# Where the "other nodes' edges" penalty of an attention maximum is added: from an activation and a fused add-and-max to a matmul that accumulates in the same bank

## The chip, the cores and the metric

The kernel runs on one core of one Trainium2 chip. A core has a matrix engine (TensorE, PE in the rows, its weight loads PEld), VectorE (DVE), ScalarE (ACT), GpSimd (POOL) and a queue engine (SyncE, SP) that issues transfers. The metric is device time in microseconds (us). Three timed runs of the kernel before gave a median of 5694.3 us, from 5691.99 to 5695.6 us.

## The reference, cut to what matters

Four graph layers run one after another on 3125 nodes and 100000 edges. The change lies in the first, which holds four rounds of attention over the edges. Each round computes, per edge, a score, and then a softmax over the edges that share a source node:

```
qi = Q[src]; kj = K[dst]
score = (qi * kj).sum(-1) + 0.1 * (edge_attr * qi[:, :RBF]).sum(-1) + logm[dst]
smax  = jax.ops.segment_max(score, src, num_segments=N)
es    = jnp.exp(jnp.minimum(score - smax[src], 20.0))
denom = jax.ops.segment_sum(es, src, num_segments=N)
alpha = es / (denom[src] + 1e-10)
```

What the change touches is `smax`: the maximum of the scores over the edges of each source node.

## The kernel before, in words

Nodes are cut into NB = 25 blocks of P = 128. The edges of a block of source nodes are stored in KT = 38 columns of 128 edges each. For every block and column there are one-hot tables in fp8: `hotT_s` (source node by edge), `hotT_d` (destination within a window, by edge) and `hot_s` (edge by source node). Gathers and sums are matmuls with these tables.

One round of attention is the function `attend`. A hardware loop in `first_part` runs it 4 times; inside a round the 25 blocks are unrolled and software-pipelined by hand, on all engines. The unit of the pipeline is a quarter of a block: `TAKE` cuts the 38 columns into 10, 10, 9 and 9. For each unit u, PE issues in this order: `keys` (three matmuls of 49 columns per edge column for the keys, three for the queries), in one unit of four `maxima`, then a `lay`, then `values` of an earlier unit (LAG = 10 units back), a second `lay`, `total` (13 units back), and in three of four units a third `lay`.

The maximum of a block is found in 10 groups of columns (`RG`: nine of 4 columns, one of 2), one `lay` on PE and one `top` on DVE each:

- ACT, `rows_in`: the block's scores, split into three bf16 parts, are one row per column and part, in `rows`.
- PE, `lay` (line 1634): for each column k a matmul with the selector `sel[:, k, :]` writes the scores of its 128 edges into all 128 partitions of a PSUM bank. So each partition (a node) sees every edge's score, 512 for a group of 4.
- ACT, `apart` (line 1711): from the one-hot table it makes `others` = BIG * hot - BIG, which is 0 where the edge belongs to the node and -BIG elsewhere. It is one activation per unit, over 3, 3, 2 and 2 groups.
- DVE, `top` (line 1776): a fused operation adds `others` to the bank and takes the maximum into `tops`; the sum itself is written to `left`.
- DVE `largest` then reduces the 10 maxima to one per node, and PE `maxima` (line 1643) hands them back to the edges.

The banks for `lay` are two, so a `lay` waits until the `top` of two groups before is done. ACT's order in a unit is `rows_in` (one unit of four), `weigh` (line 1728, 9 or 10 small activations that multiply the values by the probabilities), `key_in` (line 1701, copies the keys out of PSUM), `apart`, `probs` (one of four). SP issues four loads per block back to back (lines 1539, 1540, 1545, 1550), when the buffers come free.

A later stage, `weigh_edges` (lines 2091, 2094, 2138), finds maxima for another layer in another way: a matmul with the stationary matrix `off` (0 on the diagonal, -BIG elsewhere; made at line 1464) and the one-hot table as moving operand starts the bank, the selector matmuls accumulate on it, and DVE takes a plain maximum.

Of the kernel before, what the change touches and what calls it, by code (L numbers as in the profile page):

```python
# [9 lines left out]
ACT = mybir.ActivationFunctionType  # L10
F32 = mybir.dt.float32
BF16 = mybir.dt.bfloat16
# [4 lines left out]
AX = mybir.AxisListType.X  # L17

P = 128
N, E, H, RBF, LAYERS, G = 3125, 100000, 48, 40, 4, 32  # L20
NB = -(-N // P)
# [24 lines left out]
BIG = float(2 ** 100)  # L46
# [1439 lines left out]
K1, KH = H1, 2 * H1  # L1486


def attend(nc, c, ps, m, lists, table, near, hotT_s, hotT_d, queryp, dead, sel, acc, nmax, spill_dst):

# [5 lines left out]
    Q = len(TAKE)  # L1498
    U = Q * NB
    RG = [range(k, min(k + 4, KT)) for k in range(0, KT, 4)]  # L1500
    NR = len(RG)
    R_AT = [(8, NR), (0, 3), (3, 6), (6, 8)]
    LAG = 2 * Q + 2
    TOPS = [NR * i + R_AT[q][1] for i in range(NB) for q in (1, 2, 3, 0)]
    VB = 4
    far = m.sb("at_far", [P, 4, 3, KH], BF16)
    attr = m.sb("at_attr", [P, 2, KT, RBF])
# [2 lines left out]
    score = m.sb("at_score", [P, 3, KT])  # L1510
    sparts = m.sb("at_sparts", [P, 2, 3, KT])
    rows = m.sb("at_rows", [3 * KT, 2, P], BF16)
    others, left = m.sb("at_others", [P, 2, 12, P], BF16), m.sb("at_left", [P, 2, 4 * P])
    minus_big = m.sb("at_minus_big", [P, 1])
    tops = m.sb("at_tops", [P, 2, NR])
    mparts = m.sb("at_mparts", [P, 2, 3])
    shift = m.sb("at_shift", [P, KT])
# [1 line left out]

    val = m.sb("at_val", [P, VB, 10, 3, H1])  # L1520
    names = ["keys", "rowk", "key", "dot", "score", "split", "turned", "rows", "laid", "top", "max", "mgot", "shift", "prob",
             "h", "val", "rest", "split2", "sum", "added", "link", "minus", "others"]
    rings = [f"attr{k}" for k in range(2)] + [f"hots{k}" for k in range(2)] + [f"hotT{k}" for k in range(4)] + [
        f"far{k}" for k in range(4)]
    turned_bank = ps[:, 7, 128:192].bitcast(BF16)
    with stage(nc, "attend", *names, *rings) as (
            block, s_keys, s_rowk, s_key, s_dot, s_score, s_split, s_turned, s_rows, s_laid, s_top, s_max, s_mgot, s_shift,
            s_prob, s_h, s_val, s_rest, s_split2, s_sum, s_added, s_link, s_minus, s_others, *dmas):
        s_attr, s_hots, s_hotT, s_far = dmas[0:2], dmas[2:4], dmas[4:8], dmas[8:12]

        @block.sync
# [62 lines left out]
        def _(pe):  # L1594
# [31 lines left out]
            def lay(i, g):  # L1626
                x = NR * i + g
                if g == 0:
                    pe.wait_ge(s_rows, i + 1)
                if x >= 2:  # L1630
                    pe.wait_ge(s_top, x - 1)
                ks, bank = RG[g], ps[:, 3 + x % 2, :]
                for j, k in enumerate(ks):
                    ins = pe.matmul(bank[:, P * j:P * j + P], sel[:, k, :], rows[:, i % 2, :], start=True, stop=True)  # L1634
                ins.then_inc(s_laid, 1)

            def maxima(i):
# [29 lines left out]
            for u in range(U + LAG + 3):  # L1667
                i, q = divmod(u, Q)
# [6 lines left out]
                b = i - 1 if q else i - 2  # L1675
# [12 lines left out]
        @block.scalar  # L1688
        def _(act):
            def rows_in(i):  # L1690
                act.wait_ge(s_turned, i + 1)
                if i >= 2:
                    act.wait_ge(s_laid, NR * (i - 1))
                act.copy(rows[:, i % 2, :], turned_bank[0:3 * KT, :]).then_inc(s_rows, 1)

            def key_in(u):
                n = len(TAKE[u % Q])
                act.wait_ge(s_keys, u + 1)
                if u >= 2:
                    act.wait_ge(s_score, u - 1)  # L1700
                act.copy(key[:, u % 2, 0:n, :], ps[:, 0, 0:H1 * n].rearrange("p (j f) -> p j f", f=H1)).then_inc(s_rowk, 1)  # L1701

            def apart(i, q):

                a, b = RG[R_AT[q][0]][0], RG[R_AT[q][1] - 1][-1] + 1
                n = Q * i + (q - 1) % Q
                if n >= 2:
                    act.wait_ge(s_top, TOPS[n - 2])
                if q == 1:
                    act.wait_ge(s_rowk, Q * i + 1)  # L1710
                act.activation(others[:, n % 2, 0:b - a, :], hotT_s[:, i % 4, a:b, :], ACT.Identity, bias=minus_big[:], scale=BIG  # L1711
                               ).then_inc(s_others, 1)

            def probs(i):
                act.wait_ge(s_shift, 2 * i + 2)
                if i >= 2:
                    act.wait_ge(s_val, Q * (i - 1))
                act.activation(prob[:, i % 2, :], shift[:], ACT.Exp).then_inc(s_prob, 1)

            def weigh(i, q):  # L1720
                v = Q * i + q
                if q == 0:
                    act.wait_ge(s_prob, i + 1)
                act.wait_ge(s_h, v + 1)
                if v >= VB:
                    act.wait_ge(s_sum, v - VB + 1)
                for j, k in enumerate(TAKE[q]):
                    ins = act.mul(val[:, v % VB, j, 0, :], ps[:, 5, H1 * j:H1 * j + H1], prob[:, i % 2, k:k + 1])  # L1728
                ins.then_inc(s_val, 1)
            act.wait_ge(s_minus, 1)  # L1730
            for u in range(U + LAG + 2):
                i, q = divmod(u, Q)
                if q == 1 and 0 <= i - 1 < NB:
                    rows_in(i - 1)
                if 0 <= u - LAG - 1 < U:
                    weigh(*divmod(u - LAG - 1, Q))
                if u < U:
                    key_in(u)
                w, r = divmod(u + 1, Q)
                if 0 <= (w - 1 if r else w - 2) < NB:  # L1740
                    apart(w - 1 if r else w - 2, r)
                if q == 1 and 0 <= i - 2 < NB:
                    probs(i - 2)

        @block.vector
        def _(dve):
            link = Link(dve, s_link)
# [17 lines left out]
                link(dve.tensor_tensor(sp[:, 1, :], sp[:, 0, :], high(sp[:, 0, :]), ALU.subtract))  # L1765
                dve.tensor_tensor(sp[:, 2, :], sp[:, 1, :], high(sp[:, 1, :]), ALU.subtract).then_inc(s_split, 1)

            def top(i, q, g):
                x = NR * i + g
                n, ks, first = P * len(RG[g]), RG[g], RG[R_AT[q][0]][0]  # L1770
                w = Q * i + (q - 1) % Q
                dve.wait_ge(s_laid, x + 1)
                dve.wait_ge(s_others, w + 1)
                if x >= 2:
                    dve.wait_ge(s_top, x - 1)
                dve.tensor_tensor_reduce(left[:, x % 2, 0:n], ps[:, 3 + x % 2, 0:n],  # L1776
                                         others[:, w % 2, ks[0] - first:ks[-1] + 1 - first, :].rearrange("p k e -> p (k e)"), 1.0,
                                         -BIG, ALU.add, ALU.max, tops[:, i % 2, g:g + 1]).then_inc(s_top, 1)

            def largest(i):  # L1780
                dve.wait_ge(s_top, NR * (i + 1))
# [17 lines left out]
            def add(i):  # L1799
                dve.wait_ge(s_sum, Q * (i + 1))  # L1800
                dve.tensor_reduce(acc[:, i, :], ps[:, 6, 0:3 * H1].rearrange("p (n f) -> p f n", f=H1), AX, ALU.add
                                  ).then_inc(s_added, 1)
            dve.memset(minus_big[:], -BIG).then_inc(s_minus, 1)
            for u in range(U + LAG + 4):
                i, q = divmod(u, Q)
                if q == 1 and 0 <= i - 4 < NB:
                    add(i - 4)
                if 1 <= u <= U:
                    scores(*divmod(u - 1, Q))
                if q == 0 and 0 <= i - 1 < NB:  # L1810
                    divide(i - 1)
                if q == 1 and 0 <= i - 2 < NB:
                    shifted(i - 2)
                b = i - 1 if q else i - 2
                if 0 <= b < NB:
                    for g in range(*R_AT[q]):
                        top(b, q, g)
                if q == 0 and 0 <= i - 2 < NB:
                    largest(i - 2)

# [703 lines left out]
def first_part(nc, c, m, ps, a, x, h, tmp, table0, embs, embp, mult, logm, list1, lists, spill_dst, starts, mask, trips, base, w1,  # L2524
               dead, sel, off, second, w1_2, choice):

    table = nc.dram_tensor("table", [NP, 3 * KH], BF16).ap()
    queries = nc.dram_tensor("queries", [NP, 3 * H1], BF16).ap()
    rows_of = lambda t: t.rearrange("(b p) w -> p b w", p=P)
    acc = m.sb("acc", [P, 32, H1])  # L2530
    nmax = m.sb("nmax", [P, 32])
# [38 lines left out]
    with nc.Fori(0, LAYERS) as layer:  # L2570
        with ExitStack() as ctx0:
            t = Memory(nc, ctx0)
            near = t.sb("near", [P, NW, 3, KH], BF16)
            hotT_s, hotT_d = t.sb("at_hotT_s", [P, 4, KT, P], F8), t.sb("at_hotT_d", [P, 4, NW, P], F8)
            first = [(hotT_s[:, 0].rearrange("p k e -> p (k e)"), lists["hotT_s"][0]),
                     (hotT_d[:, 0].rearrange("p k e -> p (k e)"), lists["hotT_d"][0])]
            with ExitStack() as ctx1:
                node_rows(nc, c, ps, a, layer, h, logm[:], vec, wqk, wm, wmT, wub, wu, queryp, table, queries, acc[:], nmax[:],
                          near, first, Memory(nc, ctx1))
            attend(nc, c, ps, t, lists, table, near, hotT_s, hotT_d, queryp, dead, sel, acc, nmax, spill_dst)  # L2580
        with ExitStack() as ctx0:
            cold_softmax(nc, c, ps, "cold", Memory(nc, ctx0), list1[COLD:COLD + CAP, :], REC, (R_DST, R_SRC, None), table,
                         queries, mask, trips, (0, 5), base, acc, nmax)
        with ExitStack() as ctx0:
            node_update(nc, c, ps, h, tmp, recip[:], acc, vec, wu, Memory(nc, ctx0))
# [1062 lines left out]
```

## Time and profile before

| what | us |
|---|---|
| median of the timed runs | 5694.3 |
| the profiled execution's own time | 5691.99 |
| its span in the profile | 5690.3 |
| the four rounds of `attend`, from first to last matmul | 451.0, 448.5, 455.0, 453.7 |
| PE busy in these four | 1566.7 of 1808.2 |
| ACT busy in these four | 1466.7 |
| DVE busy in these four | 1402.0 |
| granted PE clock over the span | 0.81 |

Busy times are unions of an engine's records. Matmuls overlap in the pipeline, so the time that a matmul costs is read from the distance between the starts of two, not from its length. "idle before, releaser" says how long an engine stood still before an instruction and which other engine's work ended that; "issue" means that nothing in the profile held it.

### The profile page before, as it was taken

What the parts mean: (1) busy time and instruction counts of PE and PEld (TensorE: products, weight loads), DVE (VectorE), ACT (ScalarE), POOL (GpSimd) and SP (SyncE); (2) the same over time, 40 slices, a digit from 0 to 9 for tenths busy, and PEclk for the clock granted to TensorE, in tenths of its full rate; (3) what the DMA queues carried; (4) which work ended last, traced back from release to release, by engine and by line L of the source; (5) the groups of instructions that cost most, each with busy time, mean ns of one, the idle gap of its engine ahead of it and who ended that gap; (6) DMA issues with size and microseconds to landing.
All of it is one profiled execution on the core that took longest, in us unless ns stands there. A gap on an engine that the chain in (4) does not pass through costs nothing. (4 is left out here: it accounts for less than half of the span.)

```text
span 5690.3 us, 187291 instructions
## 1 busy us (share of the span) xinstructions
PE 4165.3 (73%) x78576; PEld 3539.3 (62%) x78576; DVE 3801.8 (67%) x8933; ACT 2695.5 (47%) x8154; POOL 2674.8 (47%) x2702
## 2 busy tenths in 40 slices
PE   6999994036666498858976987689567844978886
PEld 3555552025555388748865886588546733977786
DVE  6888875069999588668856876688585446435244
ACT  3333331036666388748865886588502424100410
POOL 2777777756666277617752764377321510000000
PEclk7666665569999699869987997899787977988897
DMA  9322222257677444344424442544165443000000
GB/s 353 79 73 73 71 69 66 53 122 204 192 198 192 118 164 156 112 101 174 159 90 130 164 156 74 147 166 158 52 111 210 145 125 101 3 9 4 4 4 10
DMA packets 480771, 652.91 MB, mean 115 GB/s; under 512 B 315712, under 2 KB 362948, under 8 KB 476693
## 3 DMA queue, kind: packets, MB, share of 16 engines
q1 hardware_dynamic: 443541, 591.08, 33.7%
q0 software_dynamic: 33856, 48.44, 3.5%
q8 instruction: 637, 10.44, 0.7%
q14 instruction: 241, 1.97, 0.1%
q10 hardware_dynamic: 2496, 0.98, 0.1%
HBM read 460.24 MB, written 180.09 MB: 113 GB/s over the span
## 5 line engine op out<-in xcount | busy, mean ns | idle before, releaser
L299 POOL DMA_INDIRECT edges<-sb_bk_rec,sb_bk_pos x782 | 782.6, 1001 | 325.2 <-issue 234.4
L1728 ACT ACTIVATE sb_at_val<-banks,sb_at_prob 128x49 f32<-128x49 f32 x3800 | 785.9, 356 | 73.3 <-PE banks L1653 66.7
L1776 DVE CUSTOM_DVE_ANT_0 sb_at_left<-banks,sb_at_others 128x512 f32<-128x512 f32 x1000 | 646.0, 661 | 231.1 <-PE banks L1634 221.8
L1613 PE MATMUL banks<-sb_near,sb_at_hotT_d 128*128 128x49 bf16 x11100 | 621.6, 185 | 71.2 <-issue 51.2
L1615 PE MATMUL banks<-sb_queryp,sb_at_hotT_s 128*128 128x49 bf16 x11400 | 637.2, 186 | 38.6 <-issue 38.6
L1613 PEld LDWEIGHTS banks<-sb_near,sb_at_hotT_d 128*128 128x128 fp8e4 x11100 | 566.8, 97 | 76.2 <-issue 69.9
L1615 PEld LDWEIGHTS banks<-sb_queryp,sb_at_hotT_s 128*128 128x128 fp8e4 x11400 | 566.3, 97 | 44.3 <-issue 43.9
L1573 POOL TENSOR_TENSOR sb_at_key<-sb_at_key,sb_at_attr 128x400 f32<-128x400 f32 (+1 forms) x400 | 373.9, 935 | 460.2 <-ACT sb_at_key L1701 448.8
L1711 ACT ACTIVATE sb_at_others<-sb_at_hotT_s,sb_at_minus_big 128x1536 bf16<-128x1536 fp8e4 (+2 forms) x400 | 535.8, 1340 | 3.9 <-DVE sb_at_tops L1776 3.9
L1653 PE MATMUL banks<-sb_near,sb_at_hotT_d 128*128 128x49 bf16 x11100 | 368.6, 187 | 70.3 <-issue 37.7
L1580 POOL TENSOR_TENSOR sb_at_val<-sb_at_val 128x490 f32<-128x490 f32 (+1 forms) x400 | 387.1, 968 | 67.3 <-ACT sb_at_val L1728 65.9
L1634 PE MATMUL banks<-sb_at_rows,sb_sel 114*128 114x128 bf16 x3800 | 383.5, 223 | 32.4 <-issue 19.4
L1582 POOL TENSOR_TENSOR sb_at_val<-sb_at_val 128x490 f32<-128x490 f32 (+1 forms) x400 | 386.1, 965 | 31.4
L1653 PEld LDWEIGHTS banks<-sb_near,sb_at_hotT_d 128*128 128x128 fp8e4 x11100 | 338.4, 98 | 93.1 <-ACT sb_at_val L1728 45.9
L1701 ACT COPY sb_at_key<-banks 128x490 f32<-128x490 f32 (+1 forms) x400 | 228.2, 570 | 274.8 <-PE banks L1615 271.7
L1664 PE MATMUL banks<-sb_at_val,sb_at_hot_s 128*128 128x147 bf16 x3800 | 348.2, 240 | 2.8 <-POOL sb_at_val L1582 2.4
L1307 POOL TENSOR_TENSOR sb_gt_msg<-sb_gt_msg 128x245 f32<-128x245 f32 (+1 forms) x175 | 238.9, 1365 | 195.1 <-DVE sb_gt_msg L1454 194.3
L1664 PEld LDWEIGHTS banks<-sb_at_val,sb_at_hot_s 128*128 128x128 fp8e4 x3800 | 287.6, 103 | 4.0 <-POOL sb_at_val L1582 3.4
L1392 ACT CAST sb_gt_hotT_d<-banks 128x512 fp8e4<-128x512 f32 x250 | 129.3, 563 | 314.9 <-PE banks L1335 312.0
L1753 DVE TENSOR_TENSOR sb_at_key<-banks,sb_at_key 128x490 f32<-128x490 f32 (+1 forms) x400 | 254.5, 636 | 34.4 <-POOL sb_at_key L1573 34.3
L2957 PE MATMUL banks<-sb_conv_parts,sb_C 128*128 128x144 bf16 x3750 | 250.1, 232 | 30.8 <-DVE sb_conv_parts L2907 30.8
L2957 PEld LDWEIGHTS banks<-sb_conv_parts,sb_C 128*128 128x128 bf16 x3750 | 248.4, 101 | 31.9 <-DVE sb_conv_parts L2907 31.9
(696 smaller groups left out, 10299.9 us busy)
## 6 DMA issues: line engine op xcount, KB each, us to landing
sb_at_attr<-attr SPq DMA_DIRECT2D x100, 760.0 KB, 7.6
sb_at_hotT_s<-rows_src_t SPq DMA_DIRECT2D x100, 608.0 KB, 5.5
sb_at_hot_s<-rows_src SPq DMA_DIRECT2D x100, 608.0 KB, 8.7
sb_at_hotT_d<-rows_dst_t SPq DMA_DIRECT2D x100, 592.0 KB, 6.9
edges<-sb_pad SPq DMA_DIRECT2D x95, 460.0 KB
sb_gt_rec<-edges SPq DMA_DIRECT2D x25, 1748.0 KB
sb_we_hotT<-rows_dst_t SPq DMA_DIRECT2D x52, 592.0 KB, 5.9
attr<-sb_gt_rec SPq DMA_DIRECT2D x25, 760.0 KB, 12.9
```

The costliest lines, as they stand in the source:

```text
L299: pool.indirect_dma_start(list1, bass.IndirectOffsetOnAxis(pos[:, t:t + 1], 0), rec[:, k, j, :], None).then_inc(sent[k], 16)
L1580: pool.tensor_tensor(x[:, 0:n, 1, :], x[:, 0:n, 0, :], halves(0), ALU.subtract).then_inc(s_rest, 1)
L1582: pool.tensor_tensor(x[:, 0:n, 2, :], x[:, 0:n, 1, :], halves(1), ALU.subtract).then_inc(s_split2, 1)
L1613: pe.matmul(ps[:, 0, H1 * j:H1 * j + H1], where, what, start=(n == 0), stop=(n == 2))
L1615: ins = pe.matmul(ps[:, 1 + u % 2, H1 * j:H1 * j + H1], hotT_s[:, i % 4, k, :], queryp[:, i, n, :], start=(n == 0), stop=(n == 2))
L1634: ins = pe.matmul(bank[:, P * j:P * j + P], sel[:, k, :], rows[:, i % 2, :], start=True, stop=True)
L1653: ins = pe.matmul(ps[:, 5, H1 * j:H1 * j + H1], where, what, start=(n == 0), stop=(n == 2))
L1664: ins = pe.matmul(ps[:, 6, 0:3 * H1], hot_s[:, i % 2, k, :], high(val[:, v % VB, j].rearrange("p n f -> p (n f)")), start=(k == 0), stop=( ...
L1711: act.activation(others[:, n % 2, 0:b - a, :], hotT_s[:, i % 4, a:b, :], ACT.Identity, bias=minus_big[:], scale=BIG).then_inc(s_others, 1)
L1728: ins = act.mul(val[:, v % VB, j, 0, :], ps[:, 5, H1 * j:H1 * j + H1], prob[:, i % 2, k:k + 1])
L1776: dve.tensor_tensor_reduce(left[:, x % 2, 0:n], ps[:, 3 + x % 2, 0:n], others[:, w % 2, ks[0] - first:ks[-1] + 1 - first, :].rearrange("p ...
L2957: return pe.matmul(ps[:, d % AHEAD, 0:3 * H], C[:, s, P * d:P * d + P], rows(s), start=(s == 0), stop=(s == NB - 1))
```

## The change

`lay` gets one more matmul per group: `off` as the stationary matrix, the block's one-hot table `hotT_s` for the columns of the group as the moving one (512 columns, or 256 in the last group). It starts the bank; the selector matmuls now accumulate onto it. The activation `apart`, its buffers `others`, `left` and `minus_big` and the semaphores `s_minus` and `s_others` go, and `top` is a plain `tensor_reduce` of the bank with max.

```diff
@@ PE, lay @@
                 ks, bank = RG[g], ps[:, 3 + x % 2, :]
+                n = P * len(ks)
+                pe.matmul(bank[:, 0:n], off[:], hotT_s[:, i % 4, ks[0]:ks[-1] + 1, :].rearrange("p k e -> p (k e)"), start=True,
+                          stop=False)
                 for j, k in enumerate(ks):
-                    ins = pe.matmul(bank[:, P * j:P * j + P], sel[:, k, :], rows[:, i % 2, :], start=True, stop=True)
+                    ins = pe.matmul(bank[:, P * j:P * j + P], sel[:, k, :], rows[:, i % 2, :], start=False,
+                                    stop=(k == ks[-1]))
                 ins.then_inc(s_laid, 1)
@@ ACT @@
-            def apart(i, q):
-
-                a, b = RG[R_AT[q][0]][0], RG[R_AT[q][1] - 1][-1] + 1
-                n = Q * i + (q - 1) % Q
-                if n >= 2:
-                    act.wait_ge(s_top, TOPS[n - 2])
-                if q == 1:
-                    act.wait_ge(s_rowk, Q * i + 1)
-                act.activation(others[:, n % 2, 0:b - a, :], hotT_s[:, i % 4, a:b, :], ACT.Identity, bias=minus_big[:], scale=BIG
-                               ).then_inc(s_others, 1)
@@ ACT, the loop over units @@
-                w, r = divmod(u + 1, Q)
-                if 0 <= (w - 1 if r else w - 2) < NB:
-                    apart(w - 1 if r else w - 2, r)
@@ DVE @@
-            def top(i, q, g):
+            def top(i, g):
                 x = NR * i + g
-                n, ks, first = P * len(RG[g]), RG[g], RG[R_AT[q][0]][0]
-                w = Q * i + (q - 1) % Q
                 dve.wait_ge(s_laid, x + 1)
-                dve.wait_ge(s_others, w + 1)
-                if x >= 2:
-                    dve.wait_ge(s_top, x - 1)
-                dve.tensor_tensor_reduce(left[:, x % 2, 0:n], ps[:, 3 + x % 2, 0:n],
-                                         others[:, w % 2, ks[0] - first:ks[-1] + 1 - first, :].rearrange("p k e -> p (k e)"), 1.0,
-                                         -BIG, ALU.add, ALU.max, tops[:, i % 2, g:g + 1]).then_inc(s_top, 1)
+                dve.tensor_reduce(tops[:, i % 2, g:g + 1], ps[:, 3 + x % 2, 0:P * len(RG[g])], AX, ALU.max).then_inc(s_top, 1)
```

PE's queue of one unit with three groups, before: the end of `keys`, then `lay`, `values`, `lay`, `total`, `lay`, and the next `keys`.

```order
L1615 MATMUL banks<-sb_queryp,sb_at_hotT_s 128x49 x3
L1634 MATMUL banks<-sb_at_rows,sb_sel 128x128 x4
L1653 MATMUL banks<-sb_near,sb_at_hotT_d 128x49 x30
L1634 MATMUL banks<-sb_at_rows,sb_sel 128x128 x4
L1664 MATMUL banks<-sb_at_val,sb_at_hot_s 128x147 x10
L1634 MATMUL banks<-sb_at_rows,sb_sel 128x128 x4
L1613 MATMUL banks<-sb_near,sb_at_hotT_d 128x49 x3
```

The same unit in the changed kernel, whose line numbers are a little different:

```order
L1612 MATMUL banks<-sb_queryp,sb_at_hotT_s 128x49 x3
L1631 MATMUL banks<-sb_at_hotT_s,sb_off 128x512
L1634 MATMUL banks<-sb_at_rows,sb_sel 128x128 x4
L1654 MATMUL banks<-sb_near,sb_at_hotT_d 128x49 x30
L1631 MATMUL banks<-sb_at_hotT_s,sb_off 128x512
L1634 MATMUL banks<-sb_at_rows,sb_sel 128x128 x4
L1665 MATMUL banks<-sb_at_val,sb_at_hot_s 128x147 x10
L1631 MATMUL banks<-sb_at_hotT_s,sb_off 128x512
L1634 MATMUL banks<-sb_at_rows,sb_sel 128x128 x4
L1610 MATMUL banks<-sb_near,sb_at_hotT_d 128x49 x3
```

Each `lay` of four matmuls has one of 512 columns ahead of it; nothing else on PE moved.

ACT's queue of three units, before: `weigh` (line 1728), `key_in` (1701), `apart` (1711), and `rows_in` (1694) once.

```order
L1728 ACTIVATE sb_at_val<-banks,sb_at_prob 128x49 x10
L1701 COPY sb_at_key<-banks 128x441
L1711 ACTIVATE sb_at_others<-sb_at_hotT_s,sb_at_minus_big 128x768
L1728 ACTIVATE sb_at_val<-banks,sb_at_prob 128x49 x10
L1701 COPY sb_at_key<-banks 128x490
L1711 ACTIVATE sb_at_others<-sb_at_hotT_s,sb_at_minus_big 128x1536
L1694 COPY sb_at_rows<-banks 114x128
L1728 ACTIVATE sb_at_val<-banks,sb_at_prob 128x49 x9
```

The same in the changed kernel, where `weigh` is line 1718, `key_in` 1702 and `rows_in` 1695:

```order
L1718 ACTIVATE sb_at_val<-banks,sb_at_prob 128x49 x10
L1702 COPY sb_at_key<-banks 128x441
L1718 ACTIVATE sb_at_val<-banks,sb_at_prob 128x49 x10
L1702 COPY sb_at_key<-banks 128x490
L1695 COPY sb_at_rows<-banks 114x128
L1718 ACTIVATE sb_at_val<-banks,sb_at_prob 128x49 x9
```

One activation of 768 to 1536 elements per unit is gone, so the next `weigh` follows `key_in` at once.

## Rows read from the trace of the kernel before

**Rows 1.** The page's first part: busy time and share of the span.

```profile
span 5690.3 us, 187291 instructions
PE 4165.3 (73%) x78576; PEld 3539.3 (62%) x78576; DVE 3801.8 (67%) x8933; ACT 2695.5 (47%) x8154; POOL 2674.8 (47%) x2702
```

**Rows 2.** Windows, first round: us; PE, PEld, DVE, ACT, POOL; clock, DMA, GB/s.

```profile
1963.50:2414.50 451.00, 392.19 (x11425) 380.90 (x11425) 350.81 (x975) 366.91 (x1201) 307.35 (x325) 0.94 0.42 151
```

**Rows 3.** Windows: a steady stretch of the first round, 2070 to 2360 us.

```profile
2070.00:2360.00 290.00, 259.13 (x7774) 253.71 (x7771) 237.33 (x663) 247.56 (x816) 208.81 (x221) 0.97 0.45 163
```

**Rows 4.** Line 1801, once per block, between 2089 and 2380 us.

```profile
L1801 DVE TENSOR_REDUCE sb_acc<-banks x18: 300/301/304, 2089.6 to 2379.4; 128x49 f32<-128x147 f32 x18
```

**Rows 5.** Waits in 2070 to 2360 us: engine, line, releaser: us, times, longest.

```profile
PE banks L1613 <- issue: 12.9, 7, 2.9
PE banks L1653 <- issue: 7.2, 5, 1.9
PE banks L1615 <- issue: 6.6, 4, 2.9
PE banks L1634 <- issue: 3.0, 3, 1.6
ACT sb_at_key L1701 <- PE banks L1615: 31.5, 34, 3.9
DVE sb_at_left L1776 <- PE banks L1634: 40.5, 55, 3.8
```

**Rows 6.** Timeline of PE in one unit: start, us, count.

```profile
2110.84 0.38 PE L1634 MATMUL banks<-sb_at_rows,sb_sel 114*128 114x128 bf16 x4
2111.06 0.92 PE L1653 MATMUL banks<-sb_near,sb_at_hotT_d 128*128 128x49 bf16 x30
2111.83 0.38 PE L1634 MATMUL banks<-sb_at_rows,sb_sel 114*128 114x128 bf16 x4
```

**Rows 7.** Timeline of PE in weigh_edges.

```profile
4183.10 0.38 PE L2091 MATMUL banks<-sb_we_hotT,sb_off 128*128 128x512 fp8e4 x1
4183.32 0.39 PE L2094 MATMUL banks<-sb_we_rows,sb_sel 114*128 114x128 bf16 x4
4183.54 0.38 PE L2091 MATMUL banks<-sb_we_hotT,sb_off 128*128 128x512 fp8e4 x1
```

**Rows 8.** Three of the page's costliest groups.

```profile
L1776 DVE CUSTOM_DVE_ANT_0 sb_at_left<-banks,sb_at_others 128x512 f32<-128x512 f32 x1000 | 646.0, 661 | 231.1 <-PE banks L1634 221.8
L1711 ACT ACTIVATE sb_at_others<-sb_at_hotT_s,sb_at_minus_big 128x1536 bf16<-128x1536 fp8e4 (+2 forms) x400 | 535.8, 1340 | 3.9 <-DVE sb_at_tops L1776 3.9
...
L1653 PEld LDWEIGHTS banks<-sb_near,sb_at_hotT_d 128*128 128x128 fp8e4 x11100 | 338.4, 98 | 93.1 <-ACT sb_at_val L1728 45.9
```

**Rows 9.** Plain maxima out of PSUM, of 1024 columns (line 2138).

```profile
L2138 DVE TENSOR_REDUCE sb_we_tops<-banks x130: 812/1214/1227, 4160.8 to 4306.6; 128x8 f32<-128x1024 f32 x104, 128x5 f32<-128x640 f32 x26
```

**Rows 10.** Windows of 2 us around one block's loads.

```profile
2216.00:2218.00 2.00, 2.00 (x81) 2.00 (x78) 1.97 (x7) 1.76 (x9) 0.75 (x1) 1.00 0.94 355
2220.00:2222.00 2.00, 1.77 (x64) 1.65 (x60) 1.97 (x6) 2.00 (x7) 1.91 (x4) 1.00 1.01 410
2222.00:2224.00 2.00, 1.45 (x38) 1.45 (x38) 0.92 (x5) 1.41 (x8) 1.92 (x3) 1.00 0.43 160
2226.00:2228.00 2.00, 2.00 (x67) 2.00 (x64) 1.83 (x11) 2.00 (x6) 1.92 (x3) 1.00 0.06 12
```

**Rows 11.** The page's DMA queue that carries instructions.

```profile
q8 instruction: 637, 10.44, 0.7%
```

**Rows 12.** A long stall of PE, and the windows from and behind it.

```profile
2148.28 0.24 PE L1613 MATMUL banks<-sb_near,sb_at_hotT_d 128*128 128x49 bf16 x2 [2.93 <-issue]
2145.00:2147.00 2.00, 0.35 (x11) 0.26 (x8) 1.76 (x4) 1.59 (x9) 1.91 (x3) 1.00 0.99 386
2147.00:2154.00 7.00, 5.72 (x108) 5.72 (x108) 2.22 (x7) 3.25 (x12) 3.51 (x4) 0.53 0.24 90
```

**Rows 13.** The end of the first round: PE waits for ACT.

```profile
2391.31 0.85 PE L1653 MATMUL banks<-sb_near,sb_at_hotT_d 128*128 128x49 bf16 x27 [1.06 <-ACT sb_at_val L1728]
```

More of the change, by code:

```diff
@@ L1486, with attend @@
 K1, KH = H1, 2 * H1
-def attend(nc, c, ps, m, lists, table, near, hotT_s, hotT_d, queryp, dead, sel, acc, nmax, spill_dst):
+def attend(nc, c, ps, m, lists, table, near, hotT_s, hotT_d, queryp, dead, sel, off, acc, nmax, spill_dst):
     TAKE = [range(0, 10), range(10, 20), range(20, 29), range(29, KT)]
@@ L1503, in attend @@
     LAG = 2 * Q + 2
-    TOPS = [NR * i + R_AT[q][1] for i in range(NB) for q in (1, 2, 3, 0)]
     VB = 4
@@ L1512, in attend @@
     rows = m.sb("at_rows", [3 * KT, 2, P], BF16)
-    others, left = m.sb("at_others", [P, 2, 12, P], BF16), m.sb("at_left", [P, 2, 4 * P])
-    minus_big = m.sb("at_minus_big", [P, 1])
     tops = m.sb("at_tops", [P, 2, NR])
@@ L1521, in attend @@
     names = ["keys", "rowk", "key", "dot", "score", "split", "turned", "rows", "laid", "top", "max", "mgot", "shift", "prob",
-             "h", "val", "rest", "split2", "sum", "added", "link", "minus", "others"]
+             "h", "val", "rest", "split2", "sum", "added", "link"]
     rings = [f"attr{k}" for k in range(2)] + [f"hots{k}" for k in range(2)] + [f"hotT{k}" for k in range(4)] + [
@@ L1527, in attend @@
             block, s_keys, s_rowk, s_key, s_dot, s_score, s_split, s_turned, s_rows, s_laid, s_top, s_max, s_mgot, s_shift,
-            s_prob, s_h, s_val, s_rest, s_split2, s_sum, s_added, s_link, s_minus, s_others, *dmas):
+            s_prob, s_h, s_val, s_rest, s_split2, s_sum, s_added, s_link, *dmas):
         s_attr, s_hots, s_hotT, s_far = dmas[0:2], dmas[2:4], dmas[4:8], dmas[8:12]
@@ L1729, in weigh @@
                 ins.then_inc(s_val, 1)
-            act.wait_ge(s_minus, 1)
             for u in range(U + LAG + 2):
@@ L1802, in add @@
                                   ).then_inc(s_added, 1)
-            dve.memset(minus_big[:], -BIG).then_inc(s_minus, 1)
             for u in range(U + LAG + 4):
@@ L1816, in _ @@
                     for g in range(*R_AT[q]):
-                        top(b, q, g)
+                        top(b, g)
                 if q == 0 and 0 <= i - 2 < NB:
@@ L2579, in first_part @@
                           near, first, Memory(nc, ctx1))
-            attend(nc, c, ps, t, lists, table, near, hotT_s, hotT_d, queryp, dead, sel, acc, nmax, spill_dst)
+            attend(nc, c, ps, t, lists, table, near, hotT_s, hotT_d, queryp, dead, sel, off, acc, nmax, spill_dst)
         with ExitStack() as ctx0:
```

## The prediction

> **What bounds the kernel now.** I read the page's first part, then windows over the rounds of `attend`, then the waits in a steady stretch, and last PE's timeline. The reader is to see first that PE leads over the whole span, 4165.3 us against 3801.8 us for DVE [rows 1], but shares over a whole span decide nothing. Inside the first round PE is busy 392.19 us of 451.00, ACT 366.91, DVE 350.81 [rows 2]: three engines close together, so the waits must say who sets the pace. In the steady stretch of 290 us ACT waits 31.5 us for PE's keys and DVE 40.5 us for `lay`, while all that PE waits for is "issue" [rows 5]. So PE is the bound there, and both engines that the change relieves are the ones that wait for it.
>
> The block is my unit. Line 1801 runs once per block; 18 of them from 2089.6 to 2379.4 us give 289.8 / 17 = 17.04 us per block [rows 4]. PE is busy 259.13 / 17.02 = 15.22 us of it [rows 3] and stands still on "issue" for 12.9 + 7.2 + 6.6 + 3.0 = 29.7 us in 19 places, 1.74 us per block [rows 5].
>
> **What PE gets.** Per group there is one matmul more. Its price isn't in `attend`, but the same operation with the same operands runs in the later stage: from its start to the first selector matmul is 4183.32 - 4183.10 = 0.22 us, and the four selector matmuls behind it take 4183.54 - 4183.32 = 0.22 us [rows 7]. That is what four selector matmuls take in `attend` without it, 2111.06 - 2110.84 = 0.22 us [rows 6]. So accumulating costs the selectors nothing and the weight load of `off` is covered, and the new matmul costs its 0.22 us whole. The last group has half the columns; I estimate 0.11 us. Per block 9 x 0.22 + 0.11 = 2.09 us; 100 blocks (25 in 4 rounds) make 209 us. As PE is the bound, this lies on the path, less what PE's own pauses give back. From below the price is the 0.055 us of one selector matmul [rows 6], which would need PE to stream 512 columns in the time of 128, and rows 7 exclude it; from above 0.44 us, if it ran at half clock.
>
> **What the removal of `apart` gives.** ACT loses 535.8 us over 400 activations, 5.4 us per block [rows 8]. In the steady stretch this is worth nothing by itself: ACT already waits for PE [rows 5]. It can only shorten PE's waits for ACT. The weight loads of `values` waited 45.9 us for `weigh` in all four rounds [rows 8], 0.46 us per block at most, and a good part of it falls at the end of a round, where it stays. I take 0.2 us per block, with 0 and 0.46 as ends.
>
> **What DVE gets.** The fused add-and-max takes 661 ns on average [rows 8], with a short accumulator read behind it. A plain maximum of 1024 columns takes 1214 ns [rows 9]; one of 512 can't take longer than that nor less than half, 607 ns. I take it as equal. DVE waits for PE anyway, 40.5 us in 290 [rows 5], and the new `top` has no second input to wait for. Zero, with the later `lay` hidden in the same way: a `lay` waits for the maximum two groups back, and that gets one more 0.22 us of room.
>
> **What PE's pauses give back.** The largest term after the new matmuls. The stalls on "issue" come once per block or a little more, at the end of the block's burst of loads: at 2216 to 2222 us the transfers run at 355 to 410 GB/s, and PE's busy time in 2 us falls to 1.77 and 1.45 us as the burst ends; at 2226 us, with 12 GB/s, it is 2.00 [rows 10]. PE's instructions come by transfers too: 637 of 10.44 MB together [rows 11]. PE has 2 x 78576 instructions [rows 1], so one transfer brings about 157152 / 637 = 247 of them (an estimate that gives PE the whole queue). I read the stalls so: a delivery of instructions gets caught behind the burst and comes late by an amount that the burst sets; PE uses up what it has and stops. Then the stall is the delay minus the time that PE spends on the instructions it holds. PE runs (7774 + 7771) / 17.02 = 913 instructions per block [rows 3], 3.7 deliveries; the new matmuls add 2.09 us to them, 0.56 us per delivery. So each stall gets shorter by 0.56 us: 19 / 17.02 = 1.12 stalls per block, 0.62 us. The ends are 0 and the whole 1.74.
>
> Here the Trainium skill speaks against my step. Its page "Advanced Engine Details and Errata", section "ISA Cache", gives lines of 16 KB with 256 instructions, as the size per transfer here suggests, and says that the cache is 32 KB but 128 KB on TensorE. With eight lines ahead a late delivery of one would not stop PE, the stalls would have another cause, and the give-back of 0.62 us would be gone; the sum would then be 62 us x 0.96 higher. The stalls of rows 10 at the burst's end speak for a shallow reserve, so I keep the step.
>
> **Clock.** In the steady stretch the granted clock is 0.97 [rows 3], so some 6% of it are at 1.2 GHz, the rest at 2.4. The clock fell behind a long stall: 2.93 us on "issue", and the 7 us from 2147 us ran at 0.53 [rows 12]. Shorter stalls will bring fewer such falls. At most 3% of 17.04 us, 0.5 us per block, is to be had; I take 0.2.
>
> **The sum.** A steady block: 2.09 - 0.62 - 0.2 - 0.2 = +1.07 us, on 24 blocks of 4 rounds: 96 x 1.07 = +103 us. The last block of a round has no `keys` beside it, and PE waits there for ACT, 1.06 us ahead of one `values` [rows 13]. Its 2.09 us are hidden, and ACT's freed 5.4 us give a little, as `values` and `weigh` alternate on one bank anyway: -1 us a round, with -4 and +2 as ends. Together +103 - 4 = +99 us. The profiled execution took 5691.99 us, span 5690.3 [rows 1], 2.3 us under the median: 5692 + 99 = 5791 us. Nothing outside `attend` changes.
>
> **Rivals.**
> 1. Nothing is given back. The stalls are a fixed price of fetching, or the burst follows PE and stretches with it. For it: "issue" names no cause. Against: the place of the stalls in rows 10. Then 96 x 2.09 - 4 = +197 us: 5889 us.
> 2. More is given back. Each stall shrinks by two deliveries' worth, 2 x 0.56 x 1.12 = 1.25 us per block, and clock and ACT as above: 2.09 - 1.25 - 0.4 = 0.44 us; 96 x 0.44 - 4 = +38 us: 5730 us. For it: how many deliveries PE holds in reserve isn't seen in any row.
> 3. Faster. It is ACT that holds PE's sequencer in the "issue" stalls, which the profile can't name, and with `apart` gone they vanish with the short waits and the falls of the clock. Place: steady blocks. Price: 2.09 - 1.74 - 0.46 - 0.5 = -0.61 us; -59 - 4 = -63 us: 5629 us. It decides from the point at which more than 2.09 us per block come back. Against: ACT itself waits 31.5 us for PE in the same stretch [rows 5], and the stalls sit at the bursts.
> 4. The new matmul hides, because `lay` had room on PE: no change, 5692 us. Rows 5 leave PE no room.
>
> **Chances.** Forecast 0.62 (own range 5755 to 5835), rival 1 0.17, rival 2 0.13, rival 3 0.04, rival 4 0.04. A measurement of this kernel can tell 0.2%, 11 us, from no change. Faster takes rival 3, 0.04; within 0.2% rival 4, 0.03; slower the rest, 0.93. The range, 5725 to 5880, reaches through rival 2 and most of the way to rival 1.
>
> **What would show it.** In the changed profile: 1000 new matmuls on the line of `off`, 0.22 us from each to the next at full clock; line 1711's activations gone and ACT idle for some 5 us more per block, waiting for PE; the block's period at 18.1 us instead of 17.04; "issue" on PE in a steady stretch near 1.1 us per block; DVE's waits for `lay` longer; the granted clock at 0.97 or above. A period near 19 us with stalls as long as before shows rival 1, one under 17 us rival 3. I am wrong in the main step if PE gets waits for an engine that it does not have now, or if PE's stalls do not shrink with the longer time between deliveries.

## The result, and the profile after

The changed kernel took 5726.4 us (median of 5 runs, 5720.83 to 5742.07) against 5691.99 us for the kernel before on the same chip: ratio 1.0069, 95% interval 1.0055 to 1.0085. It is slower, as forecast, by 34 us instead of 99. That is just inside the stated range of 5725 to 5880 us, below the forecast's own 5755 to 5835, and at rival 2's 5730. The direction and the mechanism came out; the size did not. One execution of e1 below stood apart, 6807.28 us at a granted clock of 0.56; it is in that run's median but not in its ratio.

The page's first part of the changed kernel, which answers to [rows 1]:

```profile
span 5714.5 us, 186702 instructions
PE 4266.2 (75%) x79491; PEld 3587.6 (63%) x79576; DVE 3792.0 (66%) x7929; ACT 2244.4 (39%) x7754; POOL 2676.4 (47%) x2702
```

PE has 1000 weight loads more, ACT lost 451 us of busy time, DVE 10; POOL is where it was. The windows over the first round and over the steady stretch of it answer to [rows 2, 3] (busy us of PE, PEld, DVE, ACT, POOL, then clock, DMA share, GB/s):

```profile
1963.50:2424.00 460.50, 429.35 (x11669) 395.25 (x11670) 348.99 (x724) 254.58 (x1101) 307.24 (x325) 0.97 0.41 148
2070.00:2360.00 290.00, 279.61 (x7833) 259.81 (x7831) 232.36 (x489) 169.10 (x738) 205.26 (x218) 1.00 0.43 156
```

The round grew from 451.0 to 460.5 us. From first to last matmul the four rounds grew from 1808.2 to 1847.3 us, by 39; what lies outside them, where the two kernels have the same code, took 15 us less in this execution. So single profiled executions differ by some 10 us for no reason of the change, and rounds and blocks tell more than the whole span. In the steady stretch PE is now busy 279.61 us of 290 instead of 259.13, and the granted clock is 1.00 instead of 0.97. The line that runs once per block, to be set beside [rows 4]:

```profile
L1780 DVE TENSOR_REDUCE sb_acc<-banks x18: 299/301/303, 2094.4 to 2389.5; 128x49 f32<-128x147 f32 x18
```

That is 295.1 / 17 = 17.36 us per block, where it was 17.04. The waits in the steady stretch, beside [rows 5]:

```profile
ACT sb_at_key L1702 <- PE banks L1612: 51.0, 51, 2.7
DVE sb_at_tops L1757 <- PE banks L1634: 46.7, 93, 2.2
...
PE banks L1610 <- issue: 3.5, 4, 1.1
...
PE banks L1665 <- issue: 2.6, 2, 1.6
PE banks L1654 <- issue: 2.2, 5, 0.6
...
PE banks L1612 <- issue: 1.4, 2, 0.9
...
PE banks L1634 <- issue: 0.6, 1, 0.6
```

PE's stalls on "issue" fell from 29.7 us in 19 places to 10.3 us in 14. ACT waits longer for PE, 51.0 us instead of 31.5, and DVE too, 46.7 instead of 40.5. The new matmul's price, beside [rows 6, 7], on PE's timeline (start, us, count):

```profile
2101.15 0.38 PE L1631 MATMUL banks<-sb_at_hotT_s,sb_off 128*128 128x512 fp8e4 x1
2101.37 0.39 PE L1634 MATMUL banks<-sb_at_rows,sb_sel 114*128 114x128 bf16 x4
2101.59 0.86 PE L1665 MATMUL banks<-sb_at_val,sb_at_hot_s 128*128 128x147 bf16 x10
```

0.22 us for the new one, 0.22 us for the four selectors, as read beforehand. The plain maximum takes what the fused operation took [rows 8]:

```profile
L1757 DVE TENSOR_REDUCE sb_at_tops<-banks 128x1 f32<-128x512 f32 x1000 | 653.3, 662 | 275.7 <-PE banks L1634 272.9
```

**An account per block.** For all kernels below I took 21 blocks of each of the four rounds (from the first to the 22nd start of the once-per-block line) and split PE's time by the distances between the starts of matmuls. The median distance of a line and width, summed over its matmuls, is PE's own work. What a distance has beyond its median is a stall if over 0.6 us, a short wait from 0.15 to 0.6 us, and otherwise mostly matmuls at the lower clock. "Low clock" is the time granted at 1.2 GHz per round. The last column counts otherwise: PE's idle gaps over 0.15 us that the profile puts to "issue".

| kernel | block, us | own work | stalls | short waits | rest | low clock, us | gaps on "issue" |
|---|---|---|---|---|---|---|---|
| before | 16.94 | 14.30 | 1.95 | 0.25 | 0.45 | 18.5 | 1.62 |
| changed | 17.37 | 16.34 | 0.85 | 0.10 | 0.08 | 0.2 | 0.62 |
| e2, neither | 17.22 | 14.30 | 2.13 | 0.02 | 0.77 | 32.8 | 1.77 |
| e3, half the matmul | 17.20 | 15.33 | 1.67 | 0.05 | 0.17 | 3.4 | 1.34 |
| e1, both | 17.52 | 16.34 | 0.98 | 0.09 | 0.11 | 1.7 | 0.72 |
| e4, matmul twice | 18.74 | 18.39 | 0.17 | 0.11 | 0.08 | 0.1 | 0.07 |
| e5, before, loads spread | 16.13 | 14.34 | 0.75 | 0.66 | 0.35 | 10.8 | 0.56 |
| e6, changed, loads spread | 16.71 | 16.34 | 0.22 | 0.07 | 0.08 | 0.1 | 0.06 |
| e7, neither, loads spread | 16.07 | 14.33 | 0.83 | 0.57 | 0.30 | 7.8 | 0.63 |
| e8, before, half loads | 16.06 | 14.30 | 1.03 | 0.46 | 0.26 | 5.3 | 0.36 |
| e9, changed, half loads | 17.06 | 16.34 | 0.35 | 0.24 | 0.13 | 1.0 | 0.02 |
| e10, changed, repeat | 17.42 | 16.34 | 0.90 | 0.08 | 0.10 | 1.0 | 0.65 |
| e11, as e5, repeat | 16.27 | 14.29 | 0.96 | 0.56 | 0.45 | 15.5 | 0.66 |

From before to changed: +2.04 of own work, -1.10 of stalls, -0.15 of short waits, -0.37 of the rest, together +0.43 us (+0.42 from the rounded terms), 36 us on 84 blocks. Each row is one profiled execution. The two repeats show how far such rows agree: 0.05 us per block for the changed kernel, 0.14 for e5, whose stalls differ by 0.21.

### The profile page after: what moved, and what is told of

Its sections match the earlier page's. It is cut to its first block and busy times, and to the rows that moved or that the text cites. A ratio compares the mean times of both kernels' runs of the same rounds, so it can differ in the third digit from the quotient of the medians.

```text
span 5714.5 us, 186702 instructions
## 1 busy us (share of the span) xinstructions
PE 4266.2 (75%) x79491; PEld 3587.6 (63%) x79576; DVE 3792.0 (66%) x7929; ACT 2244.4 (39%) x7754; POOL 2676.4 (47%) x2702
## 5 line engine op out<-in xcount | busy, mean ns | idle before, releaser
L1718 ACT ACTIVATE sb_at_val<-banks,sb_at_prob 128x49 f32<-128x49 f32 x3800 | 772.2, 324 | 189.9 <-PE banks L1654 182.4
L1757 DVE TENSOR_REDUCE sb_at_tops<-banks 128x1 f32<-128x512 f32 x1000 | 653.3, 662 | 275.7 <-PE banks L1634 272.9
L1610 PE MATMUL banks<-sb_near,sb_at_hotT_d 128*128 128x49 bf16 x11100 | 609.8, 184 | 36.4 <-issue 18.6
L1612 PE MATMUL banks<-sb_queryp,sb_at_hotT_s 128*128 128x49 bf16 x11400 | 624.3, 185 | 14.1 <-issue 13.9
L1610 PEld LDWEIGHTS banks<-sb_near,sb_at_hotT_d 128*128 128x128 fp8e4 x11100 | 559.8, 96 | 41.5 <-issue 34.5
L1654 PE MATMUL banks<-sb_near,sb_at_hotT_d 128*128 128x49 bf16 x11100 | 358.8, 186 | 35.7 <-ACT sb_at_val L1718 22.6
L1631 PE MATMUL banks<-sb_at_hotT_s,sb_off 128*128 128x512 fp8e4 x1000 | 369.4, 369 | 3.5 <-DVE sb_at_tops L1757 3.5
L1634 PEld LDWEIGHTS banks<-sb_at_rows,sb_sel 114*128 114x128 bf16 x3800 | 296.7, 97 | 116.3 <-issue 10.0
L1654 PEld LDWEIGHTS banks<-sb_near,sb_at_hotT_d 128*128 128x128 fp8e4 x11100 | 331.3, 97 | 44.2 <-ACT sb_at_val L1718 29.7
```

The costliest lines, as they stand in the source:

```text
L1610: pe.matmul(ps[:, 0, H1 * j:H1 * j + H1], where, what, start=(n == 0), stop=(n == 2))
L1612: ins = pe.matmul(ps[:, 1 + u % 2, H1 * j:H1 * j + H1], hotT_s[:, i % 4, k, :], queryp[:, i, n, :], start=(n == 0), stop=(n == 2))
L1654: ins = pe.matmul(ps[:, 5, H1 * j:H1 * j + H1], where, what, start=(n == 0), stop=(n == 2))
L1757: dve.tensor_reduce(tops[:, i % 2, g:g + 1], ps[:, 3 + x % 2, 0:P * len(RG[g])], AX, ALU.max).then_inc(s_top, 1)
```

## The experiments

Two questions: does PE's longer own work shrink the stalls, or does ScalarE's relief (theory A or B)? And are the stalls instructions held up by the burst of loads?

**e1: the new matmul added, everything else of the kernel before kept.**

```diff
 # lay as in the changed kernel; apart, others and the fused add-and-max stay
+                pe.matmul(bank[:, 0:n], off[:], hotT_s[:, i % 4, ks[0]:ks[-1] + 1, :].rearrange("p k e -> p (k e)"), start=True,
+                          stop=False)
```

> The kernel before with only the new matmul added to each lay; the activation apart and the fused add-and-max on VectorE stay (the penalty is added twice, which changes no maximum). Theory A: the give-back comes from PE's own work getting longer, which shortens its stalls for late deliveries of instructions; ScalarE's relief has no part. Then this is as slow as the changed kernel, 5720 to 5740 us against 5692 before, with stalls of PE near 0.7 us per block and no fall of the granted clock in steady blocks. Theory B: the give-back comes from ScalarE's and VectorE's relief (5.4 us of activation per block gone); without it the new matmul costs its full 2.09 us per block, 5790 to 5890 us.

Measured: 5744.93 us against 5695.86, ratio 1.0086, interval 1.0064 to 1.0107. The window over the steady stretch:

```profile
2070.00:2360.00 290.00, 277.38 (x7742) 257.64 (x7738) 230.60 (x648) 241.55 (x795) 203.92 (x216) 0.99 0.43 157
```

PE's waits in it:

```profile
PE banks L1615 <- issue: 3.6, 3, 1.5
PE banks L1613 <- issue: 3.1, 4, 1.1
PE banks L1668 <- issue: 2.9, 3, 1.9
PE banks L1657 <- issue: 2.2, 5, 0.6
PE banks L1637 <- issue: 0.8, 1, 0.8
```

ACT is as busy as ever, 241.55 us of 290, and yet PE's stalls are down to 12.6 us. Theory A holds. The time is 4 to 5 us above the range I gave. Between the ratios 1.0086 and 1.0069 lie 10 us for the relief of ScalarE and VectorE, and the two intervals overlap.

**e2: neither of the two.** The masking is left out, each node gets the maximum over its block's edges.

```diff
 # from the changed kernel
-                pe.matmul(bank[:, 0:n], off[:], hotT_s[...], start=True, stop=False)
...
-                    ins = pe.matmul(..., rows[:, i % 2, :], start=False, stop=(k == ks[-1]))
+                    ins = pe.matmul(..., rows[:, i % 2, :], start=True, stop=True)
```

> The changed kernel without the new matmul: neither apart nor the matmul with off, plain maximum on VectorE. It leaves out the masking, so each node gets the maximum over all edges of its block. Theory A: PE's work and stalls are as before, 1.7 to 1.8 us of stalls per block; only short waits for ScalarE go, 0.1 to 0.4 us per block, 5655 to 5685 us. Theory B: ScalarE's relief gives back some 1.7 us per block by itself, 5500 to 5550 us.

Measured: 5705.23 us, ratio 1.0012, 0.9993 to 1.0031. So less work on ACT and none more on PE is worth nothing. Theory B is dead, but A's gain of 7 to 37 us did not come either. The account suggests why: the short waits did go (0.25 to 0.02), but the stalls grew by 0.18 and the low clock from 18.5 to 32.8 us per round. Windows around one stall, and PE's row behind it on the timeline:

```profile
2116.00:2118.00 2.00, 0.00 (x0) 0.00 (x0) 0.97 (x2) 0.09 (x1) 1.51 (x2) 1.00 0.98 401
2118.00:2125.00 7.00, 6.80 (x168) 6.80 (x168) 4.07 (x9) 3.13 (x12) 3.42 (x4) 0.76 0.09 33
```

```profile
2118.20 0.23 PE L1612 MATMUL banks<-sb_queryp,sb_at_hotT_s 128*128 128x49 bf16 x3 [2.26 <-issue]
```

While the loads move 401 GB/s PE starts nothing, and behind a stall of 2.26 us the clock falls to 0.76 of full over 7 us. What PE saves in front of a delivery it waits away at it. The stalls' +0.18 by itself is within what the two executions of e5 differ by; the fall of the clock is not.

**e3: the matmul over half of each group's columns.** The masking of the other half is left out.

```diff
+                m = len(ks) // 2
-                pe.matmul(bank[:, 0:n], off[:], hotT_s[:, i % 4, ks[0]:ks[-1] + 1, :]...
+                pe.matmul(bank[:, 0:P * m], off[:], hotT_s[:, i % 4, ks[0]:ks[0] + m, :]...
...
-                    ins = pe.matmul(..., rows[:, i % 2, :], start=False, stop=(k == ks[-1]))
+                    ins = pe.matmul(..., rows[:, i % 2, :], start=(j >= m), stop=(k == ks[-1] or j >= m or j == m - 1))
```

> The changed kernel with the new matmul over the first half of each group's columns only (256 instead of 512, 128 in the last group). It leaves out the masking of the other half of the edges. PE gets 1.04 us per block. Theory A: stalls per block between those of the kernel before and of the changed one, near 1.1 us, the low clock mostly gone; block period 16.6 to 17.0 us, 5660 to 5700 us, so below the mean line between no matmul and the whole one if the clock comes back already here. Rival (the give-back is a fixed share, 80% of any added PE time): 5690 to 5710 us.

**e4: the matmul twice.**

```diff
                 pe.matmul(bank[:, 0:n], off[:], hotT_s[...], start=True, stop=False)
+                pe.matmul(bank[:, 0:n], off[:], hotT_s[...], start=False, stop=False)
```

> The changed kernel with the new matmul issued twice per group (the penalty is added twice, which changes no maximum). PE gets another 2.09 us per block. Theory A: only 0.7 us of stalls per block is left to be given back and no low clock, so 1.4 to 1.8 us per block stay: 5865 to 5905 us. Rival (a fixed share of added PE time is given back, as between before and after, where 0.35 us per block stayed of 2.09): 5755 to 5775 us.

Measured: e3 5724.22 us, ratio 1.0056, 1.0034 to 1.0077, 19 us above the 5705.23 of e2 and above both ranges given; e4 5863.02 us, ratio 1.0294, 1.0274 to 1.0314, 2 us under the range. e3's stalls shrank less than expected, to 1.67 us per block and not to some 1.1, though the low clock went as expected. The window over the steady stretch of e4, and PE's waits in it:

```profile
2070.00:2360.00 290.00, 288.90 (x7377) 254.64 (x7376) 217.52 (x447) 157.75 (x682) 190.70 (x202) 1.00 0.41 152
```

```profile
PE banks L1610 <- issue: 0.7, 1, 0.7
PE banks L1612 <- issue: 0.3, 1, 0.3
```

PE is busy 288.90 us of 290: nothing left to give back. Together with e2 and the changed kernel these are four points of one curve. The first 1.03 us of own work per block changes the block by -0.02 us, the next 1.01 us by +0.17, the last 2.05 us by +1.37. The first two steps are hardly more than the repeats differ by; the last is far clear of that. A fixed share, the rival, would have put e4 at 5755 to 5775 us; it is out. By the block e3 costs nothing over e2, by the timed runs 19 us. In the profiled executions, whose spans differ by 15.8 us, 4.5 us of these lie in the four rounds and 11.3 outside them, where the code is the same. So the first step costs between nothing and 0.2 us per block; more can't be said.

**e5, e6, e7: the loads spread over the block.** Bytes and instructions stay; attributes go first, `hot_s` second, `hotT_s` third, and `hotT_d` one unit later. e5 is from the kernel before, e6 from the changed one, e7 from e2 (no masking).

```diff
                 sp.dma_start(flat(hotT_s, i % 4), lists["hotT_s"][i]).then_inc(s_hotT[i % 4], 16)
+                if i >= 4:
+                    sp.wait_ge(s_h, Q * (i - 3) + 1)
                 sp.dma_start(flat(hotT_d, i % 4), lists["hotT_d"][i]).then_inc(s_hotT[i % 4], 16)
@@ the loop @@
                 if i < NB:
-                    first(i)
                     attributes(i)
                 if i >= 3:
                     last(i - 3)
+                if i < NB:
+                    first(i)
```

> The kernel before with the four loads of a block issued one per unit instead of back to back: attributes first, then hot_s, then hotT_s, and hotT_d one unit later. Bytes, instructions and PE's work stay. Theory A (stalls are deliveries of instructions held up behind the burst of loads): stalls fall from 1.8 to 2.0 us per block to under 0.5 and the low clock goes, a block takes 15.0 to 15.5 us (ScalarE, busy 14.55 us per block, is then close to the bound), 5540 to 5580 us. Rival (the stalls are a property of fetching this many instructions whatever the loads do): same as before, 5685 to 5705 us.

> The changed kernel with the same order of loads. Theory A: stalls from 0.85 us per block to under 0.2; a block takes 16.5 to 16.7 us, 5650 to 5670 us; so against the kernel before with the same loads the change costs 90 to 130 us, since there is nothing left to give back but ScalarE's load. Rival: 5715 to 5735 us, no effect.

> Neither apart nor the matmul with off (the masking is left out), with the loads spread. Theory A, with ScalarE near the bound in the kernel before: PE's own 14.3 us per block and little else, 14.5 to 14.8 us, 5480 to 5520 us, 40 us or more below the kernel before with spread loads. If ScalarE doesn't bind there, the two are equal within 15 us.

These three ran beside a kernel before that takes 5936.43 us, and the four behind them beside one of 5920.23 us, instead of the 5695.86 of e1 to e4. The difference lies nearly all ahead of `attend` (the last transfer of line 299 starts at 1366.3 us in e5, at 1156.6 us in the kernel before), so the ratios are compared, and the blocks. The blocks of these runs stand against a profile of the kernel before that was taken where it is fast. e5 0.9918 (0.9886 to 0.9949), e6 0.9987 (0.9968 to 1.0007), e7 0.9917 (0.9886 to 0.9948). The window over a steady stretch of e5, and PE's longest wait for an engine and on "issue" in it:

```profile
2290.00:2580.00 290.00, 269.96 (x8087) 262.88 (x8084) 257.20 (x700) 261.21 (x863) 218.80 (x232) 0.98 0.51 162
```

```profile
PE banks L1646 <- DVE sb_at_mparts L1792: 4.1, 11, 1.8
PE banks L1656 <- issue: 3.7, 2, 2.1
```

The window over the same stretch of e6, and the last of PE's three waits in it, the only one on "issue":

```profile
2290.00:2580.00 290.00, 288.18 (x8099) 268.66 (x8096) 241.41 (x505) 176.81 (x767) 215.52 (x228) 1.00 0.50 158
```

```profile
PE banks L1647 <- issue: 0.2, 1, 0.2
```

The stalls fell from 1.95 to 0.75 us per block in e5 and from 0.85 to 0.22 in e6, by the order of the loads alone, and the gaps on "issue" from 1.62 to 0.56 (0.66 in the repeat) and from 0.62 to 0.06. So the burst causes some six tenths of them in the kernel before and nearly all in the changed one. The sizes are misses. Against the 5692 us that the ranges assumed I had expected 0.973 to 0.980 for e5 and 0.993 to 0.996 for e6. e5's block was 16.13 us and not 15.0 to 15.5: stalls remained, and new short waits came (0.66 us), of which the profile puts 0.25 to VectorE. e6's 16.71 us was as expected. But against e5 it is slower by 43 us and not by the 90 to 130 expected: e5 still holds 1.76 us per block of stalls, short waits and rest, of which e6 gives back 1.39. e7 equals e5 (5878.67 and 5880.18 us), so ScalarE does not bind there either; its block of 14.5 to 14.8 us did not come, it took 16.07.

**e8, e9: the loads cut in halves.** Each load becomes two, issued some half a unit apart.

```diff
+            def half(dst, src, sem, at):
+                sp.dma_start(dst[:, 0:at], src[:, 0:at]).then_inc(sem, 16)
+                yield
+                sp.dma_start(dst[:, at:], src[:, at:]).then_inc(sem, 16)
+                yield
...
+                    at(s_h, Q * (i - 3) + 1 if i >= 4 else 0)
+                    next(load)
+                    at(s_sum, Q * (i - 4) + 2 if i >= 4 else 0)
+                    next(load)
```

> The kernel before with each of a block's four loads cut into two halves, the eight halves issued about half a unit apart (gated on PE's progress). Theory A: with no transfer in the way for more than some 1.5 us, stalls fall below the 0.75 us per block of the loads spread whole; block 15.3 to 15.9 us, ratio to the kernel before 0.980 to 0.990. Rival (spreading has done what it can; ScalarE and short waits now bind): the same as with whole loads spread, 0.990 to 0.994.

> The changed kernel with the same eight half loads. Only 0.2 us of stalls per block was left with the loads spread whole; block 16.5 to 16.7 us, ratio to the kernel before 0.995 to 1.000. Against the kernel before with half loads the changed one is then slower by 60 to 120 us, three times what it is with the loads in one burst or more.

**e10, e11: repeats beside them**, the changed kernel and e5 unaltered.

> The changed kernel unaltered, beside the others on one chip: ratio 1.005 to 1.009 as before, a block 17.3 to 17.4 us.

> The kernel before with whole loads spread, again, beside the half loads on one chip: ratio 0.990 to 0.994 if the chip doesn't matter to it.

Measured: e8 0.9877 (0.9850 to 0.9904), e9 1.0056 (1.0039 to 1.0074), e10 1.0073 (1.0044 to 1.0101), e11 0.9918 (0.9887 to 0.9949). The repeats hold: the ratios of the changed kernel and of e5 come again beside another kernel before, within their intervals. e8 is the best version of all, 0.3% below e11 beside it (5853.23 and 5870.86 us), and in its range by time; theory A's reason holds only in part. The gaps on "issue" did fall, from the 0.56 and 0.66 us of the whole loads to 0.36, but other waits came in their place: its block is 16.06 us, not 15.3 to 15.9, and its pauses over 0.6 us, 1.03 us per block, are no less than with whole loads. e9 is a miss, slower than e6. Over e8 it costs 101 us, inside the 60 to 120 expected. PE's waits in a steady stretch of e8:

```profile
PE banks L1630 <- DMA sb_at_hotT_d<-rows_dst_t: 10.5, 12, 2.3
PE banks L1670 <- ACT sb_at_val L1745: 2.8, 2, 1.5
PE banks L1660 <- DVE sb_at_mparts L1806: 1.9, 2, 1.7
PE banks L1670 <- issue: 1.9, 3, 0.9
```

Its largest wait is now for the transfer of `hotT_d`, which lands too late, not for instructions; the table counts such waits as stalls. Over all blocks it is 0.49 us in e8 and 0.24 in e9, where the gaps on "issue" are down to 0.02. So the halves lessen the instructions' delay and bring another one, and a kernel with the halves and an earlier `hotT_d` was not run. With a block's loads spread whole, the change costs 0.9987 / 0.9918, 0.7%; with half loads 1.0056 / 0.9877, 1.8%, against 0.7% with the burst.

## Why the prediction was right or wrong

- **PE is the bound; relief of ACT and DVE is worth nothing by itself.** Right: e2.
- **The new matmul: 2.09 us per block.** Right: 2.04, with 0.22 us each. But the sum divides it among the deliveries of before, 0.56 us each. The new matmuls bring instructions of their own: 14.30 us of own work for 904 instructions are 4.05 us per 256, 16.34 us for 924 are 4.53, so a delivery of 256 lasts 0.48 us longer.
- **`apart` gives back 0.2 us per block in short waits.** The short waits went by 0.15, but e1 shows 0.16 of the 0.25 going with `apart` still there; it was more PE's own slack than ACT's relief.
- **The maximum on DVE: equal.** Right, 662 ns for 661.
- **Stalls: -0.62 us per block. This is the step that failed, in its size.** Measured -1.10. The mechanism, a delivery held up by the burst while PE uses what it holds, is shown by e1 and by e5 and e6. What failed is the sum on it: every stall of before shorter by one delivery's 0.56 us, and nothing more. The number of stalls fell from 24.5 to 16.5 per round and their mean from 1.67 to 1.08 us. That the mean lost 0.59 us looks like the 0.56 of the forecast, but does not confirm it, as stalls that fall below 0.6 us leave the mean. With 0.56 us taken off each of the stalls of before one by one, 19.0 per round would stay above 0.6 us, with a mean of 1.33 us, 1.21 us per block; measured were 0.85 and, in the repeat, 0.90. With twice 0.56 us taken off, 11.25 would stay, 0.59 us per block. So, if the delays themselves were as before, a stall gave back more than one delivery's worth and less than two. Short stalls that go altogether can't be the reason, since each gives back less than the full 0.56. That in a burst of fixed length PE comes to the end of its instructions less often when each lot lasts longer is an argument and was not tested; the cause of the surplus stays open.
- **Clock: -0.2 us per block.** Too small as well: low clock went from 18.5 to 0.2 us per round, and the rest in the table by 0.37. With the shorter stalls the falls were all but gone (1.0 us in the repeat). In the changed kernel the longest stall of these blocks, 1.62 us, has none behind it, as its row on the timeline and the windows around it show:

```profile
2138.32 0.59 PE L1665 MATMUL banks<-sb_at_val,sb_at_hot_s 128*128 128x147 bf16 x6 [1.62 <-issue]
```

```profile
2136.00:2138.50 2.50, 0.88 (x12) 0.64 (x11) 0.70 (x2) 2.03 (x10) 2.26 (x4) 1.00 0.98 385
2138.50:2146.00 7.50, 7.50 (x214) 7.01 (x213) 5.70 (x12) 3.12 (x12) 4.49 (x5) 1.00 0.23 85
```

- **The last block hides its matmuls.** Right within 1 us: from the 22nd to the last start of the once-per-block line it takes 35.3 us before and 35.4 after.
- The sum: forecast 2.09 - 1.02 = 1.07 us, measured 2.04 - 1.62 = 0.42. Two give-backs, stalls and clock, were each taken too small, by 0.48 and, if the rest is all clock, by 0.17 us.
- **Rival 1** (nothing is given back) fell with the result and with e1; that the stalls are no fixed price of fetching is e5 and e6. **Rival 2** has the time, and its reason in part: its 1.25 us of stalls per block is nearer to the measured 1.10 than the forecast's 0.62, but two deliveries' worth off each stall is more than was given back. That its sum meets the measured time is in part luck. **Rival 3** fell with e2. **Rival 4**'s 5692 us is excluded by the interval.
- **The objection in the prediction.** The page "Advanced Engine Details and Errata" of the Trainium skill, section "ISA Cache", has lines of 256 instructions; the trace agrees with that, as the last section shows. The same section also says "Only 2 cache lines!", which the prediction left out when it held the 128 KB on TensorE, eight lines, against itself. The runs bear out the small reserve: a delivery late by a few us stops PE.

## What to carry to other kernels

Work added to a saturated engine does not cost its length if that engine also waits for its own instructions: the first microsecond per block cost at most 0.2 us here, the last two cost two thirds of their length. So measure the stalls by what surrounds them, large transfers above all, before pricing a change; and fix the order of the transfers first, since e8, with the old computation and no burst, beats the kernel before by 1.2% and the changed one by 1.9%.

## What the runs showed that I had not expected

In the stretch below, PE's stalls in the kernel before lie at fixed distances in its instruction stream. Windows from one stall to the next in the kernel before (the counts are matmuls and weight loads):

```profile
2222.50:2235.08 12.58, 12.52 (x380) 12.34 (x380) 10.86 (x33) 11.89 (x41) 9.53 (x11) 1.00 0.34 120
2239.56:2253.60 14.04, 12.33 (x387) 12.03 (x384) 11.78 (x34) 11.99 (x41) 9.35 (x11) 1.00 0.38 138
2253.60:2271.80 18.20, 16.62 (x513) 16.33 (x509) 15.19 (x43) 16.39 (x54) 14.22 (x17) 1.00 0.48 168
2271.80:2285.52 13.72, 12.24 (x387) 11.94 (x384) 12.09 (x34) 11.94 (x41) 9.63 (x11) 1.00 0.44 157
```

384 weight loads with their matmuls are 768 instructions, 3 x 256; 512 with theirs are 1024, 4 x 256 (a window may cut a few records at its ends). In the records of ten stalls that end between 2222 and 2359 us, nine of them over 0.6 us, PE resumed 1.3 to 1.5 us after a 16 KB packet of the instruction queue had landed. The same holds for all 83 gaps on "issue" over 0.6 us in the 84 blocks of the kernel before (1.20 to 1.60 us) and for the 39 of the changed one (1.21 to 1.57 us). And the packets that ended these gaps came behind the burst: in the 3 us before the packet's start the transfers ran at over 300 GB/s for 77 of the 83 and for all 39, against 35% of all instruction packets in these blocks before and 36% after. That ties a stall to a late delivery more closely than its place beside a burst.
